# Pacing the indirect sends of layer 1's expert routing, and moving its expert stretch 38 attention slots later

## The reference, cut to what matters

```python
    # 8 sequences of 512 tokens, 128 wide: 4096 tokens
    xn = _layernorm(x, axis=-1)
    s = _L1_attn_ref(xn, wq, wk, wv, wo, pope_bias)    # 16 heads of 8, softmax over 512 keys
    g = _silu(_L1_ffn_ref(xn, ln_weight, router_w, w1, w3, w2))
    x = x + s * g

def _L1_ffn_ref(hidden_states, ln_weight, router_w, w1, w3, w2):   # 8 experts, top 2, FFN 352
    x = _rms_norm(hidden_states, ln_weight, EPS).reshape(b * s, h)
    probs = jax.nn.softmax(x @ router_w, axis=-1)
    top_p, top_i = jax.lax.top_k(probs, TOP_K)
    gates = jnp.sum(jax.nn.one_hot(top_i, N_EXPERTS, dtype=x.dtype) * top_p[..., None], axis=1)
    h1 = jnp.einsum('td,edf->tef', x, w1)
    h3 = jnp.einsum('td,edf->tef', x, w3)
    y = jnp.einsum('tef,efd->ted', jax.nn.silu(h1) * h3, w2)
    out = jnp.einsum('te,ted->td', gates, y)
```

## Time and profile before

| | us |
|---|---|
| median of 3 runs | 1522.78 |
| lowest and highest of them | 1521.34, 1527.52 |
| the profiled execution | 1517.4 |
| its span, first to last instruction | 1515.4 |

### The profile page before, as it was taken

The page is one execution under the profiler, slowest core; times in us unless marked ns, Lnnn a source line. Parts: engine busy times, 40 slices in busy tenths (PEclk is TensorE's granted clock), DMA queues, the critical chain, the costliest instruction groups (busy, mean ns, idle before and its releaser), DMA issues.

```text
span 1515.4 us, 16091 instructions
## 1 busy us (share of the span) xinstructions
PE 1003.4 (66%) x5318; PEld 535.5 (35%) x5318; DVE 914.8 (60%) x1426; ACT 652.1 (43%) x966; POOL 544.2 (36%) x548
## 2 busy tenths in 40 slices
PE   5352377787777125277541579999977787778784
PEld 5121144444444012132210127888623232323231
DVE  6640577656565236988831465666577676767771
ACT  3210254555445032145420454344446565656574
POOL 6377125767663242661167030000224040404210
PEclk9865678989889555578665779999978888888898
DMA  8512434565643525413121344666343333333300
GB/s 260 197 51 77 126 91 118 153 162 139 167 125 112 67 53 72 65 34 43 25 63 53 46 98 147 204 197 193 108 72 53 54 56 51 56 51 57 64 16 14
DMA packets 90764, 143.57 MB, mean 95 GB/s; under 512 B 17721, under 2 KB 48058, under 8 KB 90682
## 3 DMA queue, kind: packets, MB, share of 16 engines
q1 hardware_dynamic: 82010, 124.97, 35.3%
q0 software_dynamic: 8192, 16.79, 4.4%
q10 hardware_dynamic: 480, 0.79, 0.4%
HBM read 58.17 MB, written 40.37 MB: 65 GB/s over the span
## 4 chain that ended last, share of the span: by engine, by line
PE 26%; DVE 10%; ACT 8%; DMA 6%; issue 6%; another core or an unknown queue 6%; SPq 3%; POOL 1%; ACTq 0%; DVEq 0%; POOLq 0%
PE PS L911 7%; ACT P L978 5%; PE PS L870 4%; PE PS L930 4%; DMA KS<-MAG 4%; SPq L484 3%; PE PS L888 3%; DVE MX L1682 3%; PE PS L850 3%; PE PS L834 2%; PE PS L668 1%; PE PS L673 1%; DMA YG<-Y0D,POS 1%; ACT MAG L978 1%
## 5 line engine op out<-in xcount | busy, mean ns | idle before, releaser
L1682 DVE TENSOR_REDUCE MX<-PS 128x2 f32<-128x1024 f32 x256 | 306.3, 1222 | 189.7 <-PE PS L850 123.0
L978 ACT ACTIVATE P<-PS 128x1024 f32<-128x1024 f32 x256 | 262.3, 1025 | 262.8 <-PE PS L888 177.2
L888 PE MATMUL PS<-QS,KS 64*128 64x512 f32 x512 | 130.0, 504 | 146.0 <-ACT P L978 84.5
L850 PE MATMUL PS<-KS,QS 62*128 62x512 f32 x512 | 144.9, 564 | 64.0 <-DVE MX L1682 40.7
L1276 POOL DMA_INDIRECT A<-Y1D,POS x64 | 74.1, 1158 | 279.2 <-DMA Y1D<-YE 186.9
L870 PE MATMUL PS<-P,V 128*32 128x512 f32 x1024 | 162.0, 710 | 0.1
L850 PEld LDWEIGHTS PS<-KS,QS 62*128 62x128 f32 x512 | 55.6, 214 | 214.7 <-issue 102.2
L888 PEld LDWEIGHTS PS<-QS,KS 64*128 64x128 f32 x512 | 56.2, 215 | 199.2 <-ACT P L978 120.9
L1302 POOL TENSOR_TENSOR MAG<-MAG,EH 128x1024 f32<-128x1024 f32 x7 | 16.5, 2356 | 277.2 <-ACT MAG L978 277.1
L911 PE MATMUL PS<-XRH,WH 128*128 128x512 f32 (+1 forms) x276 | 104.8, 422 | 0.0
L767 PE MATMUL PS<-XST,WB 128*128 128x512 f32 x184 | 99.7, 684 | 0.0
(11 more groups left out here) (212 smaller groups left out, 1842.8 us busy)
## 6 DMA issues: line engine op xcount, KB each, us to landing
WH<-W1SD SPq DMA_DIRECT2D x23, 704.0 KB, 4.7
WS<-WD SPq DMA_DIRECT2D x64, 200.0 KB, 4.2
QS<-EH SPq DMA_DIRECT2D x64, 128.0 KB
KS<-EH SPq DMA_DIRECT2D x60, 128.0 KB
WB<-in_wb SPq DMA_DIRECT2D x23, 322.0 KB, 2.9
XS<-XS0D SPq DMA_DIRECT2D x23, 256.0 KB, 4.1
Y0D<-YE SPq DMA_DIRECT2D x23, 256.0 KB, 4.2
XS<-XS1D SPq DMA_DIRECT2D x23, 256.0 KB, 4.1
```

What stands on the lines that cost most here:

```text
L850: signal(pe.matmul(PS[:, s % 4, :], QS[rows, u % 3, hp, 128 * t:128 * t + 128], KS[rows, u % 3, hp, :], start=True, stop=True), "ms")
L888: signal(pe.matmul(PS[:, 4 + s % 2, :], KS[rows, u % 3, hp, 128 * k:128 * k + 128], QS[rows, u % 3, hp, :], start=True, stop=True), "st")
L978: act.activation(*a, **k).then_inc(sem[name], 1)
L1682: go("mx", dve.tensor_reduce(MX[:, u % 2, t].rearrange("p (o h) -> p o h", o=2)[:, :, hp], PS[:, s % 4 - 1:s % 4 + 1, :], AX.X, ALU.max))
```

## The change

Each of the 64 sends becomes an item of its own, one in each of the slots 58 to 121, where 32 items of two sends stood in slots 58 to 89. Before it issues, POOL waits until `mx` has reached 56 + n for send n, so until the row maxima of slot 55 + n are done. `BLOCKS_AT` goes from 92 to 130: the expert stretch, its weight loads (slot 121 for 83), its first rows (129 for 91) and the gathers of sequences 0 to 2 (slots 131, 139, 147 for 93, 101, 125) come later, and items of slots 92 to 129 now take the shifts that end in `_first`. DVE waits in `route` part 0 for a count of `one_free` which its own last `logitsev` has brought about.

```diff
-BLOCKS_AT = 92
+SEND_AT = ROUTE_AT + ROUTE_PARTS + 1
+BLOCKS_AT = 130
@@
-    for g in range(TILES):
-        put(ROUTE_AT + ROUTE_PARTS + 1 + g, ("send", g))
+    for n in range(2 * TILES):
+        put(SEND_AT + n, ("send", n))
@@
                 elif what == "send":
-                    g = a[0]
-                    if g == 0:
+                    n = a[0]
+                    g, k = divmod(n, 2)
+                    if n == 0:
                         pool.wait_ge(sem["pos1"], 2)
-                    for k in range(2):
-                        pool.indirect_dma_start(XS1D, bass.IndirectOffsetOnAxis(POS[1][:, k, g:g + 1], 0), XN[:, g, :],
-                                                None).then_inc(sem["sent1"], 16)
+                    pool.wait_ge(sem["mx"], SEND_AT + n - 2)
+                    pool.indirect_dma_start(XS1D, bass.IndirectOffsetOnAxis(POS[1][:, k, g:g + 1], 0), XN[:, g, :],
+                                            None).then_inc(sem["sent1"], 16)
@@
                     if a[0] == 0:
                         dve.wait_ge(sem["h"], B)
+                        dve.wait_ge(sem["one_free"], 1 + max(SHARED["logits", b] for b in range(B)))
```

## The result

| | before | after |
|---|---|---|
| median of 4 runs each, us | 1524.53 | 1461.41 |
| lowest and highest | 1521.34, 1527.52 | 1457.29, 1464.39 |
| ratio of the times, 95% interval | | 0.9584 [0.9552, 0.9617] |
| the profiled execution | 1517.4 | 1464.39 |
| its span | 1515.4 | 1462.0 |

The change takes 63.1 us (4.2%) off the medians; the forecast was -62 us and 1461 us. That holds for the chip of this comparison. On three other chips the kernel before took about 1416 us, and on the one of them that also ran the changed kernel (1410.36 us against 1415.08) the two can't be told apart. The experiments come to that, and it is the most important thing in this document.

What follows compares the result with a forecast made beforehand. News of PE's work reaching other engines 13 to 30 us late beside dense sends was taken to bound layer 1's empty stretch; -66.7 - 4 + 0 + 7 + 2 = -62 us gave 1461 us, range 1443 to 1497.

Steps and rivals of the forecast that it cites:

- The stall and its size: Layer 1, slots 57 to 90: dense sends delay the news of PE's work; spacing them saves 66.7 us.
- No gather in that stretch: Slots 57 to 90 hold no gather, unlike slots 153 to 186 used for comparison: -4 us, bounds 0 and -8.
- A paced send: Layer 1's 64 sends, one per slot: the waits they still cause, +7 us in all, range 0 to +29.
- the paused gathers: Gathers about 2 us apart, 1230.31 to 1239 us, no "remote" wait among the longest: a spaced send's cost from below, 0.
- The moved gathers: Gathers of sequences 0 to 2 move to slots 131 to 147: same number, so 0, up to +5 us.
- The seam: In front of the experts, sends end earlier but `minus` copies precede the first rows: +2 us, bounds -5 and +5.
- The shifts ending in `_first`: Valid in only one of slots 57 to 90 and slots 153 to 186; claimed to cost nothing.
- DVE's wait: In `route` part 0, the added wait asks for a count that DVE's own `logitsev` has made true: 0.
- A: Each spaced layer 1 send holds PE's signals a little, 0.77 us, 49 us for 64: 1503 us; chance 0.11.
- B: Cost belongs to each send, not its density (1528 us), or the stall has its own cause (1523 us); chance 0.07.
- C: Each send meets a signal on the critical ring; loses from 1.08 us per send, 1550 us at 1.5; chance 0.04.
- The signs that I had named: Sends 2.3 us apart from about 762 to 910 us, slots 57 to 90 in 75 to 90 us, layer 0's stall unchanged.

## Why the prediction was right, step by step

**The stall and its size.** Right. 66.7 us too long by the twin; 65.8 us went (80.6 against 146.4), and with the sends taken out altogether 67.5 (78.9). That is for chips with holds. The link of the hold to the sends, which I had from coincidence in time alone, is shown by three runs: it goes without the sends, stays away with other POOL work in their place, and returns with the burst at another place of the expert stretch.

**No gather in that stretch**, taken -4: measured -0.7 (78.9 against 79.6). I had halved the 7.8 us excess behind the expert stretch; nearly all of it belongs to that place.

**A paced send**, taken +7 for 64: 1.7 us for 34, so about +3. The two misses cancel: -4 + 7 against -0.7 + 3. That the forecast landed 1.1 us from the measured difference is in part luck: the cuts without start and tail give -61.0 us, and single executions spread over 7 us. The row that decided was the paused gathers; the groups that I priced at 3.6 us did come (seven sends from 765.56 to 773.25 us, five at most behind them); the "remote" waits beside them were of 3.1 us and less, as the earlier trace rows had it.

**The moved gathers**, taken 0, up to +5: slots 92 to 129 became 10.7 us shorter and slots 130 to 255 13.1 us longer, +2.4. On the chips without holds it was -1.7 + 11.1 = +9.4, outside my bound. "Their number is the same" was not enough of a reason. On both sorts of chips 7.5 to 7.7 us of the loss stand in slots 130 to 139, right behind the stretch; that a gather there meets a DVE that comes to its sum before it has landed is seen once (7.1 us on chip 3) and doesn't cover it, so the cause isn't shown. The run with pacing undone says +11.7 us for the whole move by its median, and +9.9 by the cuts of its own trace (-6.9, +14.9 and +1.9 at the seam), against 2.4 + 2.4 by those of the changed kernel. So this step's bound of +5 was too narrow on the chip with holds too; the term is small enough that the sum held.

**The seam**, taken +2: +2.4. **The shifts ending in `_first`** and **DVE's wait**: nothing of theirs shows.

**The rivals.** A (0.77 us per send) and B (the cost belongs to the send, or has its own cause) fall with 0.05 us per paced send. C, slower from 1.08 us per send, too: its send tied to a row maximum met no long wait, and the wait on `mx` is also what keeps the queue short. The signs that I had named came: sends 2.29 us apart from 765.6 to 909.7 us, 80.6 us for the stretch, layer 0's stall in place.

**What no step had.** I took the profile for that of the kernel; it was that of the kernel on one sort of chip. My steps would have given 0.96 on chip 3 as well, where it is 0.9971. The single profile didn't say so, but the unnamed releaser "remote" was a warning that I read only as a puzzle of names. And the second cost of the burst, `mag` behind 58 sends in POOL's queue, was hidden under the hold: on a chip with holds the slots are so late that `mag` isn't.

Two pages of the Trainium skill spoke against the stall. "SBUF — State Buffer", section "SBUF: two separate sides", says that a DMA can't slow a compute op or the other way round. On chips 11, 3 and 8 no row contradicts it. On chip 14 the sends cost the computing engines waits of up to 27.7 us, but the sentence is about an operation itself, and that isn't slower (a row maximum takes 1.22 us with and without): what comes late is the news between engines. "TensorE: Matmul & The Clock Gate", section "The cost: per-tile semaphore tail", gives 26.3 ns for one more increment; beside the burst on chip 14 the measured delay is a thousand times that.

## What to carry to other kernels

A long burst of indirect DMAs that POOL issues has two prices: on some chips, at least while the profile is recorded, the engines hear of PE's work tens of us late beside it, and whatever POOL must compute next stands behind it (15.0 us of waiting on chip 8, where no hold hid it). Tie such sends to the progress of the work around them, with a wait on a counter which that work advances anyway: this spaces them and keeps the queue short, which the fixed spacing of 2.40 us didn't. When a profile shows idle time with a releaser that has no name, look at the same kernel on other chips before the gain is counted; and when work is moved, ask who stands at its new place, not whether its amount is the same.

## What the runs showed of the hardware

- The same kernel takes 1416 us on three chips and 1520 to 1524 us on chip 14 and in the comparison. Between the two traces of the kernel before, 84.4 of the 102.5 us lie where the "remote" waits are: 31.9 up to slot 57 (763.1 against 731.2), with layer 0's sends in it, and 52.5 from slot 57 to 91 (146.4 against 93.9). The other 18.1 us, with "remote" waits of 4.5 us and less in them, were not taken apart.
- The two sorts differ in one more thing in their traces. Where there are holds, the page gives no time to landing for the copies of `EH`, nor for layer 0's indirect DMAs; where there are none, it does (2.2 us for the sends). For layer 1's indirect DMAs neither has one. The same line of the page, of the kernel before, on the comparison's chip and on chip 8:

```profile
QS<-EH SPq DMA_DIRECT2D x64, 128.0 KB
```

```profile
QS<-EH SPq DMA_DIRECT2D x64, 128.0 KB, 4.2
```

- Semaphore events, from which that time is worked out, are recorded only in part there. The 64 sends of a layer make 1024 of them, 16 each. Of layer 0's the packed trace of the kernel before holds 235 on the comparison's chip and all 1024 on chip 8; of layer 1's 211 and 1018. And they go missing with the hold: of layer 1's there are 219 with pacing undone, 605 in the changed kernel and 950 with the fixed spacing (the first and the last on chip 14).
- Every run on record has a span and a granted clock, so every timed execution here was also a recorded one. So it stays open whether such a chip holds signals by itself, or the recording of events does it there. That events are lost just where signals are late makes the recording a suspect, and with it the 4.2%; only a timing without recording could tell, and none was made.
- What is late is the increment, as far as its recorded event tells. The scores end at 805.62 us, the event of the semaphore that ACT waits for stands at 826.47 us, and ACT starts at 826.49. Whether plain DMAs do the same stays open.
- The granted clock followed the idle time. Slots 57 to 91 ran at 0.69 with the hold and 0.83 without it; on the other chips 0.78 with the wait for `mag` and 0.87 without. In the stretch with the hold PE was busy for 64.8 us, in the changed kernel for 60.5 with the same matmuls, so a stall's cost includes slower matmuls beside it.
